# A three-stage decoder kernel on one core: bounces through memory split into a write and reads on one queue, and the steps of all engines in a new order

## What is computed

```
x = layernorm(x + attention(x))            # causal local attention, 16 heads of 16, plus 50 latent
                                           # tokens (4 heads), mixed by a sigmoid gate
x = layernorm(x + cross_attention(x, ctx)) # q and k normalized per head, 361 keys
x = layernorm(x + experts(x))              # top-1 routing, 8 experts, 200 places each
```

```
attn = softmax(einsum('bhqd,bhkd->bhqk', layernorm(qh) * scale, layernorm(kh)))
x = einsum('bhqk,bhkd->bhqd', attn, vh)
```

## Time and profile before

| | us |
|---|---|
| median of three runs (1562.82 to 1567.44) | 1565.06 |
| the profiled execution's own time | 1558.71 |
| its span | 1556.9 |
| TensorE busy (77%) | 1203.6 |
| VectorE busy (53%) | 831.7 |
| ScalarE busy (43%) | 669.1 |
| GpSimd busy (22%) | 335.0 |

### The profile page before, as it was taken

How to read it: one execution, slowest core, us unless ns; L and a number is a source line. 1 busy time by engine, 2 the same in 40 slices (tenths; PEclk the granted TensorE clock), 3 DMA queues, 4 the chain that set the end, 5 groups by cost and what they waited for, 6 DMA issues and landing times.

```text
span 1556.9 us, 33968 instructions
## 1 busy us (share of the span) xinstructions
PE 1203.6 (77%) x11098; PEld 873.9 (56%) x11098; DVE 831.7 (53%) x2482; ACT 669.1 (43%) x1611; POOL 335.0 (22%) x485
## 2 busy tenths in 40 slices
PE   3577877877888888888878888888878887775886
PEld 2354555555555555555555656565555555554774
DVE  4235555555655565555556555555555555543432
ACT  0124544445545444444445544444455454532110
POOL 2111221222222222222222222222222222210111
PEclk8668999999999999999999999999999999876998
DMA  4233333333333333333333333333333333206542
GB/s 157 47 80 83 83 73 86 86 75 84 81 71 78 75 83 76 84 84 84 84 84 84 80 73 82 72 84 84 78 77 81 71 78 74 66 18 214 194 148 72
DMA packets 187012, 134.99 MB, mean 87 GB/s; under 512 B 95798, under 2 KB 182762, under 8 KB 186734
## 3 DMA queue, kind: packets, MB, share of 16 engines
q1 hardware_dynamic: 181778, 127.50, 33.5%
q0 software_dynamic: 3200, 6.61, 1.4%
q10 hardware_dynamic: 1984, 0.23, 0.1%
HBM read 91.06 MB, written 43.00 MB: 86 GB/s over the span
## 4 chain that ended last, share of the span: by engine, by line
PE 38%; DMA 28%; SPq 9%; issue 9%; DVE 7%; POOL 4%; ACT 4%; DVEq 0%; POOLq 0%; ACTq 0%
DMA query_halves<-Qhl 8%; DMA self_stack<-self_halves 8%; DMA self_halves<-QKhl 6%; DMA Qst<-query_halves 5%; PE MI L1006 4%; POOL QKhl L701 4%; PE MI L809 4%; SPq L574 4%; PE MX L1123 4%; PE MI L810 3%; PE MX L837 3%; PE ST L993 3%; SPq L590 3%; PE MX L843 2%; PE ST L870 2%
## 5 line engine op out<-in xcount | busy, mean ns | idle before, releaser
L1427 DVE TENSOR_REDUCE negmax_x<-MX 100x1 bf16<-100x361 f32 x512 | 260.0, 532 | 123.8 <-PE MX L975 119.1
L1192 ACT ACTIVATE wide<-ST 128x800 f32<-128x800 f32 (+1 forms) x256 | 171.0, 669 | 222.7 <-PE ST L993 221.9
L975 PE MATMUL MX<-stacked,Qst 96*128 96x361 f16 x512 | 152.1, 327 | 40.3 <-DMA Qst<-query_halves 29.9
L707 POOL TENSOR_TENSOR Qhl<-Qx,Qhl 128x400 f16<-128x400 f32 x32 | 30.2, 944 | 695.0 <-ACT Qhl L1264 695.0
L837 PE MATMUL MX<-mask_q,identb 100*128 100x400 bf16 (+1 forms) x128 | 57.1, 547 | 93.8 <-DMA self_stack<-self_halves 92.4
L993 PE MATMUL ST<-Qst,stacked 112*128 112x200 f16 x768 | 124.5, 278 | 0.3 <-ACT wide L1192 0.3
L975 PEld LDWEIGHTS MX<-stacked,Qst 96*128 96x128 f16 x512 | 50.7, 102 | 101.8 <-issue 54.7
L701 POOL TENSOR_TENSOR QKhl<-QK,QKhl 128x900 f16<-128x900 f32 x32 | 60.5, 1891 | 204.9 <-ACT QKhl L1199 204.9
L1154 ACT ACTIVATE early<-MI,bkC 128x361 f32<-128x361 f32 x64 | 36.0, 562 | 148.8 <-PE MI L810 145.5
L993 PEld LDWEIGHTS ST<-Qst,stacked 112*128 112x128 f16 x768 | 72.5, 109 | 41.2 <-issue 26.2
L1398 DVE TENSOR_SCALAR QK<-MI,small,parity_s 128x100 f32<-128x100 f32 x128 | 42.6, 374 | 76.9 <-PE MI L810 72.9
(11 more groups left out here) (259 smaller groups left out, 2918.4 us busy)
## 6 DMA issues: line engine op xcount, KB each, us to landing
stacked<-key_halves SPq DMA_DIRECT2D x96, 180.5 KB, 4.1
self_halves<-QKhl SPq DMA_DIRECT2D x32, 450.0 KB, 2.9
cT<-in_cT SPq DMA_DIRECT2D x32, 361.0 KB, 4.0
key_halves<-Khl SPq DMA_DIRECT2D x32, 361.0 KB, 2.7
self_stack<-self_halves SPq DMA_DIRECT2D x64, 150.0 KB, 3.9
Qst<-query_halves SPq DMA_DIRECT2D x96, 100.0 KB, 2.6
early<-in_w SPq DMA_DIRECT2D x8, 1024.0 KB
self_stack<-self_halves SPq DMA_DIRECT2D x32, 225.0 KB, 3.8
```

The costliest lines, as they stand in the source:

```text
L975: pe.matmul(MX[:, n % 2, 0:M], Qst[p][0:96, n * S:n * S + 128], Kst[p][0:96, n // 2 * M:(n // 2 + 1) * M], start=True, stop=True).then_inc ...
L1192: act.activation(cross_part(Px, u), ST[0:n, first:first + 2, 0:width], ACT.Exp).then_inc(st_exp, 1)
L1427: dve.tensor_reduce(negmax_x[:, n:n + 1], MX[0:S, n % 2, 0:M], X, ALU.max, negate=True).then_inc(max_read, 1)
```

## The change

The write and the reads of a bounce become two functions (`bounce_self`, `bounce`, and `stack_self`, `stack`), with the waits divided between them. On SP's queue other transfers come between the two for keys and queries. The self bounce now opens SP's iteration, and the loads of the context, of x and of the rows move behind it.

```
-            def stack_self(it):
+            def bounce_self(it):
                 a = it.of("A")
...
                 sp.dma_start(self_halves.rearrange("h p n -> p h n"), QKhl[:]).then_inc(a_out, 16)
+
+            def stack_self(it):
+
+                a = it.of("A")
...
-            def stack(it, b, target, source, halves, order, made, count_made, out, stacked):
+            def bounce(b, source, halves, made, count_made, out, stacked):
...
                 sp.dma_start(halves.rearrange("h p n -> p h n"), source[:]).then_inc(out, 16)
+
+            def stack(it, b, target, source, halves, order, out, stacked):
+
                 there, free = held(sp, b.done(per=16)), held(sp, in_order(SCORES, "Y7", it) if it.has("Y") else 0)
...
             def body(it):
+                if it.has("A"):
+                    bounce_self(it)
+                    stack_self(it)
+                if it.has("K"):
+                    bounce_keys(it)
+                if it.n + 2 < B:
+                    load_c(Seq(it.n + 2, it.j))
                 if it.n + 3 < B:
                     load_x(Seq(it.n + 3, it.j))
+                if it.has("B"):
+                    bounce_queries(it)
                 if it.n + 2 < B:
                     load_n(Seq(it.n + 2, it.j))
-                if it.has("A"):
-                    stack_self(it)
                 if it.has("K"):
                     stack_keys(it)
-                if it.n + 2 < B:
-                    load_c(Seq(it.n + 2, it.j))
                 if it.has("B"):
                     stack_queries(it)
```

On the other four engines no step is added, removed or altered; their order is. GpSimd:

```
-                if a: pair_sums(A)
-                if b: gate_local(Bs, it)
-                if a: self_lo(it)
-                if b: gate_remote(Bs, it); mix(Bs); query_low(it)
+                if a: pair_sums(A); self_lo(it)
+                if b: gate_local(Bs, it); gate_remote(Bs, it)
                 if t: keep_x2(T)
-                if b: x1_bias(Bs)
+                if b: mix(Bs); x1_bias(Bs); query_low(it)
                 if t: scatter(T)
```

```
-                if k: key_low(it, 0)
-                if x: cross_max(it, 11); cross_max(it, 12)
+                if x: cross_max(it, 9); cross_max(it, 10); cross_max(it, 11)
                 if k: key_norm(it, 0)
...
-                if b: rstd(it.of("B"), rs1, ln1, mv1, b_ln, b_rs)
-                if a: A4(it)
+                if a: A4(it)
+                if t: router_exp(it)
```

More of the change, by code:

```diff
@@ L1058, in body @@
+                if y: cross_scores(it, 0)
+                if t: T2(it)
+                if y: cross_scores(it, 1)
+                if x: cross_maximum(it, 0); cross_maximum(it, 1)
+                if k: K12(it, 0)
+                if y: cross_scores(it, 2)
+                if x: cross_maximum(it, 2); cross_maximum(it, 3); cross_maximum(it, 4)
+                if b: B1(it)
                 if t: T3(it)
+                if y: cross_scores(it, 3)
                 if x: cross_maximum(it, 5)
                 if b: B2(it)
-                if y: cross_scores(it, 3)
@@ L1080, in body @@
+                if y: cross_scores(it, 7)
+                if a: A4(it)
+                if t: T5(it)
+                if x: cross_maximum(it, 13)
                 if v: V56(it, [0, 1])
+                if t: T6(it)
+                if x: cross_maximum(it, 14)
+                if a: self_scores(it, 0)
                 if b: B5(it)
[L1082 to L1085 removed]
+                if a: self_scores(it, 1)
@@ L1594, in body @@
                 if a: self_max(it, 1)
+                if k: key_norm(it, 1)
                 if t: route_to(it)
                 if x: cross_max(it, 13)
-                if k: key_norm(it, 1)
+                if k: key_low(it, 0)
                 if b: norm1(it)
-                if x: cross_max(it, 14); cross_max(it, 15)
+                if t: place_in(it)
+                if x: cross_max(it, 14)
                 if k: key_low(it, 1)
-                if t: place_in(it)
+                if x: cross_max(it, 15)
                 if b: queries(it)
+                if y: Y2(it)
                 if a: A7(it)
-                if y: Y2(it)
             iterations(dve, body)
```

87 lines of the change are left out of this document (39 added, 48 removed).

## The result

| | before | after |
|---|---|---|
| median of 20 runs, us | 1562.93 | 1546.60 |
| ratio, with its 95% interval | 1 | 0.9885 [0.9862, 0.9908] |
| the profiled execution's own time, us | 1558.71 | 1558.85 |
| its span | 1556.9 | 1557.0 |
| TensorE busy | 1203.6 | 1211.0 |

The changed kernel is faster by 1.15%, about 18 us by the ratio and 16 by the medians; 60 were forecast. (The median is of all 20 runs; the ratio leaves out five slower ones of the kernel after, the profiled one and one of 1816.93 at a granted clock of 0.61 among them.) 1546.6 lies in the upper part of the range given, in the band of the second rival. Its profiled execution lies 12 us above its median: from 164.76 to 294.50 three iterations took 129.7 us where three of before took 120.8, one of them with a wait of 4.27 for x.

The account below looks back on a forecast made before the run. No engine but a chain of waits in three legs bounds the 40.74 us iteration. Legs of 12.9, 12.9 and 12.3 make 38.1, plus 0.7 for the clock 38.8; over 31 intervals this saves 60 us: 1505, range 1490 to 1525.

Parts of the forecast that it names:

- the second rival: The clock falls as now, or x's late load keeps A1 back: 1545 us, or 1565 for no change; chance 0.22.
- The self strand: Self bounce from A1's start to the self maxima As0: 18.1 us, getting earlier and going off the path.
- Leg 1: From the first cross maximum X0 to the self maxima As0: bound by VectorE's reductions, 12.9 us, bounds 12.4 to 13.8.
- Leg 2: From As0 to the end of B7: 12.3 us with the clock up, 14.3 with it down.
- A1 at 7.3: TensorE's A1 starts 7.3 us after B7, waiting about 1 us for x's load behind the context load.
- Leg 3: From B7's end to X0: 12.9 us, upper end 13.5, query reads landing 1.2 us after the key reads.
- X0's own place costs nothing: On TensorE, A1 to X0 takes 4.7 us, so TensorE reaches X0 at 12.0 us after B7.
- The clock in one iteration of three: TensorE's clock falls in one iteration of three, adding 0.7 us to 38.1 per iteration.
- The sum: Main-loop iteration of 38.8 us against 40.74, saving 1.95 in each of 31 intervals, 60 us: 1505 us.
- the third: Rival: key reads hold back the query reads on SP's queue, X0 15.0 us after B7, slower at 1608 us; chance 0.13.

Follow-up runs that it names:

- e11: Kernel after with SP's queue order of before, but the query write ahead of the context load, plus extra TensorE passes ahead of X0 and X10 to X12: 1433.38 us.
- e9: Kernel after plus extra TensorE passes whose result nobody reads, ahead of X0 and X10 to X12, none at A1: 1523.66 us.
- e3: Kernel after with SP's queue order of the kernel before, so the new order of the other engines alone: 1517.16 us.
- e5: Kernel after with x's load moved right behind the self reads and the key reads right behind the key write: 1518.73 us.
- e2: Kernel after with only x's load moved, to right behind the self reads, ahead of the key write: 1564.59 us.
- e4: Kernel before with only SP's queue order changed to that of the kernel after: 1658.90 us.
- e6: Kernel after plus extra TensorE passes: five ahead of A1's wait for x, others ahead of X0 and X10 to X12: 1653.10 us.
- e1: Kernel after with only the key reads moved, right behind the key write, ahead of the context, x and query write: 1568.18 us.
- e7: e3 plus extra TensorE passes, 7 ahead of X0 and thin ones ahead of X10 to X12, none at A1: 1468.45 us.
- e12: e11 without any extra passes, the kernel after with SP's order alone altered: 1459.33 us.

## Why the prediction went wrong

By its steps, in its order:

- **The self strand**: right. 18.1 from A1 to As0 was worked out; 18.23 is measured in e11, in the one iteration where As0 waited for it. After, As0 waited three times in twenty, 1.5 us in all.
- **Leg 1**: right. 12.9 was forecast; with the clock up it is 12.6 to 12.9. The reductions behind K1 and T3 (X2 and X5) waited 0.90 and 0.86 for 1.0 each, gate_sum 0.24 for 0.5; VectorE's timeline of after:

```profile
770.43 1.50 DVE L1445 TENSOR_REDUCE negmax_x<-MX 100x1 bf16<-100x361 f32 x3 [0.90 <-PE MX L991]
772.78 0.54 DVE L1445 TENSOR_REDUCE negmax_x<-MX 100x1 bf16<-100x361 f32 x1 [0.86 <-PE MX L991]
...
776.36 0.42 DVE L1466 TENSOR_REDUCE gate_z<-gate_t 100x16 f32<-100x256 f32 x1 [0.24 <-POOL gate_t L711]
```

- **Leg 2**: right. 12.3 and 14.3 were forecast for the two levels of the clock; 12.0 with the clock up (12.03 on average in e9), and 12.6 to 14.4 with a fall in it.
- **A1 at 7.3**: 7.62 on average, 7.3 to 8.2. Right, in the upper half of what was named (6.6 to 7.9), but for one iteration. (The terms named beside the 7.9, 3.5 and 4.0, make 7.5.)
- **Leg 3**: this term failed, and with it the forecast. It was 14.24, not 12.9, and its bounds of 12.2 to 13.5 did not hold it either. The steps up to the last read's issue were right: in the iteration above, B7 ended at 754.27, the query write went out 5.24 later (5.0) and landed in 3.2 (3.2 to 3.8), and the third query read went out some 9.9 after B7 (9.5 to 10.2). What was mis-sized is the price of standing behind the key reads. I let the keys land at 11.7 and gave the query reads another 1.2, at most 1.8. The key reads themselves became slower, 4.7 for 4.1, which puts their end at about 12.5 (the last out at 762.1, 7.8 after B7), and the query reads need some 1.4 beyond that (X0 at 13.93 here). The sum had costed the slower query reads and left the key reads at the price that they have ahead of the context and the query write (4.1 in before, e3 and e5; 4.6 to 4.8 behind both in e2, e4, e6 and e9). e1 shows that the place behind the key reads is what costs: without it the query reads land in 2.6.
- **"X0's own place costs nothing"**: wrong in eight of the twenty iterations. The 4.7 from A1 to X0 was taken from a row at full clock, and 4.62 is what it takes there; the clock that falls behind A1's wait makes it 6.1 to 7.7. In these eight X0 comes 14.4 after B7 on average, in the other twelve, where the query reads set it, 14.1.
- **The clock in one iteration of three**: wrong, and it hardly shows. 21 falls in 20 iterations were counted. Legs 1 and 2 together are 25.97; 24.7 with the clock up (e9), so it costs 1.3, not 0.7. But the legs without it were 0.5 shorter than forecast (24.7 for 25.2), so that 25.97 meets the 25.9 that the text had summed. That is luck: two errors cancel.
- **The sum**: 40.21 for 38.8. Of the 1.4 missing per iteration, 1.3 is leg 3. Over 31 intervals 1.4 is 43, and 1505 + 43 = 1548; the median is 1546.6. How closely these agree is luck in part: the legs are those of the profiled execution, which took 12 us more than the median. It lost 9 us in the three iterations named above, and 256 us passed behind its last As0 where before has 249.5, a stretch that the prediction took as unchanged. (With the new order of the engines the other kernels have 248 to 255.5 there.)
- **The rivals**: the third had the right mechanism, at some 60% of its price: X0 at 14.2 rather than 15.0 after B7 (1.3 more than forecast, not 2.1), with leg 1 hardly longer, and so a smaller gain and not a loss. It had named 13.6 (the clock falls there) and 14.9 (leg 1 stays) as the points of decision; 14.2 lies between. That its key reads would pass "in a wait that is there anyway" was the reason against it, and e1, e3 and e5 show that it was not good enough. The second's A1 held back by x came in as well, by less; what neither said is that x's wait, by the clock behind it, would bring TensorE to X0 as late as the query reads do, so that only removing both (e5) helps.

What stays open: why the clock falls at As0 in some iterations of the kernel after and not in others. The passes ahead of X0 and X10 to X12 end these falls, but they were not tried one by one. Nor was it tried whether the 7.4 us of e6 go with the length of the program or with the place A1; 28 extra passes in an iteration (e7), none of them at A1, are free of it, 32 (e6) are not.

## What to carry to other kernels

Splitting a write from its reads so that other transfers go out in between fills the queue's wait, but it also puts their bytes in front of the reads; what the path needs soonest should have the least in front of it, in write and reads alike (e11: 113 us below the kernel after, 87 of them by the queue's order alone, e12). A change that does two things is best priced in its four combinations: here one part won 46 us and the other lost 29. And where taking one wait away gives nothing, look at a second strand that ends at the same place, and at the clock behind the waits that are left, before calling the first one harmless.

## What the runs showed of the hardware that was not expected

- The clock can fall where TensorE waits for no transfer, at As0 after a thinly used stretch (TensorE busy 2.23 of 3.50 in the row of 654.50, then 0.50 in that of 658.50), and extra passes in such places are cheaper than the falls: with 27 of them in an iteration the time went down by 23 us (e9), with 28 by 49 (e7).
- A loop with five more passes in an iteration stood 7.4 us (4.8 + 2.6) in every round of two iterations, with some nine packets of instructions, 16 KB each, in a round, where the kernel after and e9 move none in the loop. Packets and waits fall together in every round; it looks like program code fetched anew, but that the waits are for it is not shown.
- Reads of 300 KB behind 541 KB of other reads in the same queue landed 1.7 us later than alone. The reads in front were slower too, 4.7 for 4.1, but they had also moved behind the context's load and the query write; what of the two slowed them was not tried.
